# A fused attention and top-2 expert kernel: front reordered, gates and send counts moved into the expert stage, one chain of weight scales, tables read from PSUM

## The reference

```python
xn = _layernorm(x)                      # no scale, no shift, eps 1e-5
# attention, one head, causal, within each batch: q = xn Wq^T + bq, k = xn Wk^T + bk, v = xn Wv^T + bv
# experts:
logits = xn @ Wr + br
probs = softmax(logits)                 # over the 16 experts
topv, topi = top_k(probs, 2)
h = relu(xn @ W1[e] + b1[e])
y = h @ W2[e] + b2[e]
out = x + attention(xn) + sum over the two chosen e of topv * y
```

## Time and profile before

| what | us |
|---|---|
| median of 3 executions | 175.81 |
| lowest, highest | 175.55, 177.71 |
| the profiled execution, its own time | 176.07 |
| its span in the trace | 174.3 |

### The profile page before, as it was taken

The page is one execution under the profiler, slowest core; times in us unless marked ns, Lnnn a source line. Parts: engine busy times, 40 slices in busy tenths (PEclk is TensorE's granted clock), DMA queues, the critical chain, the costliest instruction groups (busy, mean ns, idle before and its releaser), DMA issues.

```text
span 174.3 us, 4762 instructions
## 1 busy us (share of the span) xinstructions
PE 154.9 (89%) x1418; PEld 136.1 (78%) x1418; DVE 113.1 (65%) x447; ACT 114.3 (66%) x337; POOL 99.9 (57%) x149
## 2 busy tenths in 40 slices
PE   5888789998769996989999999999999899987990
PEld 5764444768757855979999999989999799987670
DVE  1589666789997787857988854545453543532772
ACT  3478967897658956119999768786877567464000
POOL 7646888888888886000655565655464645635700
PEclk9999999999999999999999999999999999999999
DMA  5579999610111651154464521001100000003946
GB/s 143 147 262 408 405 406 407 229 46 32 49 47 37 176 139 47 46 127 109 118 151 114 138 78 49 15 9 36 47 32 21 26 30 29 29 34 116 301 140 181
DMA packets 22416, 21.60 MB, mean 124 GB/s; under 512 B 3589, under 2 KB 16211, under 8 KB 22392
## 3 DMA queue, kind: packets, MB, share of 16 engines
q1 hardware_dynamic: 19864, 17.06, 31.1%
q0 software_dynamic: 2528, 4.24, 7.0%
HBM read 14.94 MB, written 7.32 MB: 128 GB/s over the span
## 4 chain that ended last, share of the span: by engine, by line
PE 57%; DVE 19%; issue 8%; DMA 7%; ACT 4%; SPq 1%; POOL 1%; DVEq 0%; POOLq 0%
PE pOO L1201 21%; PE pOO L1093 6%; PE pS L1188 6%; PE pS L1065 6%; PE pS L1190 5%; PE pS L1189 5%; DMA w<-pairs_dram 3%; PE pT L1156 3%; DVE pS L795 3%; DMA pairs_dram<-ybuf,pair 2%; PE pT L1078 2%; DMA xin<-in_L_attn_x 2%; PE pS L986 1%; DVE xin L909 1%; SPq L377 1%
## 5 line engine op out<-in xcount | busy, mean ns | idle before, releaser
L454 POOL DMA_INDIRECT pairs_dram<-ybuf,pair x47 | 46.5, 988 | 50.2 <-DVE ybuf L883 35.9
L580 ACT ACTIVATE xT<-pS,b1t 128x128 f32<-128x128 f32 x188 | 55.1, 406 | 23.1 <-PE pS L1190 22.4
L1201 PE MATMUL pOO<-w,xT 128*128 x376 | 52.0, 282 | 1.0 <-DVE ybuf L883 1.0
L1201 PEld LDWEIGHTS pOO<-w,xT 128*128 128x128 f32 x376 | 45.6, 192 | 1.2 <-issue 1.2
L446 POOL DMA_INDIRECT slots_dram<-rows,slotrow x32 | 31.6, 986 | 9.7 <-POOL tick L448 8.6
L1188 PE MATMUL pS<-xT,w1hi 128*128 128x128 f16 x188 | 33.9, 219 | 1.7 <-DVE xT L876 1.2
L1190 PE MATMUL pS<-xT,w 128*128 128x128 f16 x188 | 33.9, 219 | 0.0
L1189 PE MATMUL pS<-xT,w1hi 128*128 128x128 f16 x188 | 33.9, 219 | 0.0
L875 DVE CAST xT<-pT 128x128 f16<-128x128 f32 x47 | 13.7, 291 | 30.4 <-PE pT L1156 26.8
L1188 PEld LDWEIGHTS pS<-xT,w1hi 128*128 x188 | 21.3, 113 | 3.0 <-DVE xT L876 1.8
L1093 PE MATMUL pOO<-v,probsT 128*128 128x128 f32 x144 | 19.5, 281 | 4.0 <-DVE xin L814 3.6
(11 more groups left out here) (169 smaller groups left out, 230.9 us busy)
## 6 DMA issues: line engine op xcount, KB each, us to landing
w<-in_L_ffn_W SPq DMA_DIRECT2D x8, 1024.0 KB, 8.1
slots<-slots_dram SPq DMA_DIRECT2D x47, 65.0 KB, 1.9
w<-pairs_dram SPq DMA_DIRECT2D x8, 256.0 KB, 4.4
slots_dram<-slots SPq DMA_DIRECT2D x16, 65.0 KB
...
pairs_dram<-ybuf,pair POOLq DMA_INDIRECT x47
slots_dram<-rows,slotrow POOLq DMA_INDIRECT x32
```

The costliest lines, as they stand in the source:

```text
L454: pool.indirect_dma_start(pairs_dram, bass.IndirectOffsetOnAxis(ap=pair[:, j:j + 1], axis=0), ybuf[:, j % NYB, :], None, bounds_check=NT * ...
L580: ins = nc.scalar.activation(hid[:, j % NHB, here], pA(j)[:, here], ACT.Relu, bias=b1t[:, c, j:j + 1])
L1201: ins = pe.matmul(pO[r % 2][:, 0:D], hid[:, r % NHB, c * P:(c + 1) * P], second_weights(r, c), start=(c == 0), stop=(c == NCH - 1))
```

## The change

Front: the normalising of a group is dealt out by tables over ACT, POOL and DVE (group 0: ACT one tile, POOL one, DVE two; group 1: ACT and POOL two each; groups 2 and 3: ACT and DVE two each). On ACT xT_copy(0) moves ahead of std_of(1), qk_copy(1) ahead of xT_copy(1), and qk_copy(3) and v_copy(3) behind the first softmax. On PE project_qk(1) moves ahead of x_transposes(1), project_qk(2) and (3) ahead of x_transposes(2), values(3) behind scores(1), ranks(1), (2), (3) to steps 0, 1 and 5 of the attention, behind attend. On DVE moments(2) moves behind choose(0), inverse_std(2) behind rank(0), logits(3) and rank(1) into the attention. choose(g) loses a conversion and compares the unsigned indices themselves.

Attention: `carry(t)` comes behind `attend(t)`. The weight scales are one chain for 16 experts in step 11 instead of two chains for 8 in steps 7 and 12. hidden_biases and factor_rows are both in step 14; DVE multiplies the biases straight from PSUM (no copy b1raw). Some TENSOR_SCALAR with a scalar from memory become TENSOR_TENSOR with a broadcast. first_rows stands ahead of row_max in step 7.

Experts: the gates leave the attention: DVE subtracts the maxima (`gaps`) in pass 13, ACT takes the exponentials in pass 14, DVE makes the gates in pass 15 and the send counts (`sent_tiles`) in pass 16; ACT's diagonals begin one pass later. LOW_LATE begins with pass 0. SP waits for slotrow_done instead of gates_done, and for sent_done ahead of the counts. lg, oh, at and ex get tiles of their own.

```diff
-    SG = 8
-    WARM_UP = 14
-    ACT_NORMS = 2
+    WARM_UP = 7
+
+    ACT_TILES = [(0,), (0, 1), (0, 1), (0, 1)]
+    POOL_TILES = [(1,), (2, 3), (), ()]
+    DVE_TILES = [(2, 3), (), (2, 3), (2, 3)]
+
+    GATES = 13
+    DIAGS = GATES + 4
 
...
-        SQUARES = {0: (0,), 1: (1,), 2: (2,), 3: (3, 4), 4: (5,), 5: (6, 7), 6: (8, 9), 7: (10, 11), 8: (12,), 9: (13,),
-                   10: (14,), 11: (15,)}
-        HIGH = {8: (0,), 9: (1,), 10: (2,), 12: (3,), 13: (4,)}
-        LOW = {9: (0,), 11: (1,), 13: (2,), 14: (3,)}
+        SQUARES = {0: (0,), 1: (1,), 2: (2,), 3: (3, 4), 4: (5, 6), 5: (7, 8), 6: (9, 10, 11), 7: (12, 13, 14, 15)}
+        HIGH = {12: (0,), 13: (1, 2), 14: (3, 4)}
+        LOW = {13: (0,), 14: (1, 2)}
 
         HIGH_LATE = {j: (j + 5,) for j in range(E - 5)}
-        LOW_LATE = {j: (j + 3,) for j in range(1, E - 3)}
+        LOW_LATE = {j: (j + 3,) for j in range(E - 3)}
 
 
...
-                for t in range(G * g + ACT_NORMS, G * g + G):
+                for t in (G * g + i for i in POOL_TILES[g]):
...
             normalise(0)
+            xT_copy(0)
+            std_of(1)
             act.wait_ge(wT_done, 2)
             nc.scalar.copy(wqkT[:, :, :], pA(2)[:, 0:2 * D].rearrange("p (n d) -> p n d", n=2)).then_inc(wT_copied, 1)
-            std_of(1)
-            xT_copy(0)
             normalise(1)
-            std_of(2)
             v_copy(0)
-            xT_copy(1)
             act.wait_ge(bqk_in, 32)
             qk_copy(0)
+            qk_copy(1)
+            xT_copy(1)
+            std_of(2)
             v_copy(1)
             normalise(2)
-            qk_copy(1)
             xT_copy(2)
             std_of(3)
             qk_copy(2)
             normalise(3)
             v_copy(2)
-            qk_copy(3)
             xT_copy(3)
 
             nc.scalar.activation(loaded[:, :], ident[:, 0:1], ACT.Exp)
-            v_copy(3)
 
             def squares(e):
...
             softmax(0)
+            qk_copy(3)
+            v_copy(3)
+            softmax(1)
             qk_copy(4)
-            softmax(1)
+            probsT_copy(0)
             qk_copy(5)
...
+                if j == GATES + 1:
+                    exponentials()
+                if j == DIAGS:
                     act.wait_ge(gates_done, 1)
-                if E <= j < E + K * NDIAG:
-                    k, t = (j - E) % K, (j - E) // K
+                if DIAGS <= j < DIAGS + K * NDIAG:
+                    k, t = (j - DIAGS) % K, (j - DIAGS) // K
...
-                step(dve.tensor_copy(pickf[:, here, :], pick[:, here, 0:K]))
-                dve.tensor_copy(rows_i[:, here, D + 1], pickf[:, here, 0])
+                dve.tensor_tensor(rows_u[:, here, D + 1], pick[:, here, 0], pick[:, here, 0], ALU.bitwise_or)
                 for k in range(K):
                     ins = dve.tensor_tensor(oh[:, k, here, :], expert_no[:, None, :].broadcast_to([P, G, E]),
-                                            pickf[:, here, k:k + 1].broadcast_to([P, G, E]), ALU.is_equal)
+                                            pick[:, here, k:k + 1].broadcast_to([P, G, E]), ALU.is_equal)
...
             moments(0)
             inverse_std(0)
+            normalise(0)
             moments(1)
             inverse_std(1)
-            moments(2)
             dve.wait_ge(brb_in, 16)
             dve.wait_ge(consts, 1)
             logits(0)
             largest(0)
             choose(0)
-            inverse_std(2)
+            moments(2)
             logits(1)
             rank(0)
+            inverse_std(2)
+            normalise(2)
             moments(3)
             largest(1)
             inverse_std(3)
-            normalise(NG - 1)
+            normalise(3)
             logits(2)
             choose(1)
-            logits(3)
-            rank(1)
 
...
+            def gaps():
+                dve.tensor_tensor(ex[:, :, :], lg[:, :, :], top[:, :, 0:1].broadcast_to([P, NT, E]), ALU.subtract)
+                dve.tensor_tensor(gap[:, :], top[:, :, 1], top[:, :, 0], ALU.subtract).then_inc(gap_done, 1)
...
             row_max(0)
             row_max(1)
+            logits(3)
             largest(2)
             probsT_copy(0)
             row_max(2)
+            choose(2)
             for t in range(NT - 1):
                 if t >= 1:
                     inverse_sum(t - 1)
                     attended(t - 1)
                 probsT_copy(t + 1)
+                if t == 7:
+                    first_rows()
                 if t + 3 < NT:
                     row_max(t + 3)
                 if t == 0:
-                    choose(2)
+                    rank(1)
                 if t == 1:
+                    rank(2)
+                if t == 2:
                     largest(3)
-                if t == 2:
-                    rank(2)
-                if t == 3:
+                if t == 4:
                     choose(3)
-                if t == 4:
+                if t == 5:
                     rank(3)
-                if t == 5:
                     tiles_of_experts()
-                    sent_tiles()
                 if t == 6:
                     experts_of_tiles()
-                    first_rows()
                 if t == 7:
-                    scales(0)
-                if t == 8:
                     rows_of_tiles()
-                if t == 10:
-                    bias_table()
-                    gates()
+                if t == 11:
+                    scales()
                 if t == 12:
-                    scales(1)
-                    dve.wait_ge(scale_done, E // SG)
+                    dve.wait_ge(scale_done, 1)
                     factors()
-                if t == 13:
-                    factor_tables()
                 for e in LOW.get(t, ()):
                     low(e)
+            factor_tables()
             for t in range(NT - LAST, NT):
                 inverse_sum(t)
...
+                if j == GATES:
+                    gaps()
+                if j == GATES + 2:
+                    gates()
+                if j == GATES + 3:
+                    sent_tiles()
...
             values(0)
-            x_transposes(1)
             pe.wait_ge(wT_copied, 2)
             project_qk(0)
-            values(1)
+            project_qk(1)
+            x_transposes(1)
             pe.wait_ge(consts, 1)
             ranks(0)
-            project_qk(1)
+            values(1)
+            project_qk(2)
+            project_qk(3)
             x_transposes(2)
-            project_qk(2)
             values(2)
-            project_qk(3)
             x_transposes(3)
-            values(3)
-            ranks(1)
 
             def tile_rows(bank):
...
                 if t < 2:
-                    project_qk(6 + t)
-                if t == 2:
-                    ranks(2)
-                if t == 4:
+                    ranks(t + 1)
+                if t == 5:
                     ranks(3)
-                if t == 6:
+                if t == 7:
                     pe.wait_ge(total_read, 1)
-                    weight_sums(0, bank)
-                if t == 8:
-                    pe.wait_ge(scale_done, 1)
                     tile_rows(bank)
                 if t == 10:
                     pe.wait_ge(erow_done, 1)
                     pe.wait_ge(onehot_done, 1)
+                    weight_sums(bank)
+                if t == 14:
+                    pe.wait_ge(scale_done, 1)
                     hidden_biases(bank)
-                if t == 12:
-                    pe.wait_ge(b1_read, 1)
-                    weight_sums(1, bank)
-                if t == 13:
-                    pe.wait_ge(scale_done, 2)
                     factor_rows(bank)
...
             scores(0)
             scores(1)
+            values(3)
             project_qk(4)
-            project_qk(5)
             probs_transposes(0)
             scores(2)
+            project_qk(5)
             for t in range(NT - 1):
                 probs_transposes(t + 1)
                 if t + 3 < NT:
                     scores(t + 3)
-                carry(t)
+                if t < 2:
+                    project_qk(6 + t)
                 if t < NT - LAST:
                     attend(t)
+                carry(t)
 
             ids = {}
```

120 lines of the change are left out of this document (51 added, 69 removed).

## The result

Four runs of the changed kernel took 178.7 to 181.27 us, median 181.01; the kernel before, in the same session, 175.55 to 177.71, median 176.25. The ratio is 1.023, with a 95% interval of 1.012 to 1.034. The forecast was 177.6 with a range up to 179.0. The profiled run took 181.27, its span is 179.5.

What follows compares the result with a forecast made beforehand. PE's attention and POOL's strictly serial sends were taken to end together at 74.1, PE bounding the expert stage. Span 174.3 + 0.7 + 1.1 = 176.1, plus 1.77 around it 177.9, less 0.26: 177.6 us; range 175.2 to 179.0.

Steps and rivals of the forecast that it cites:

- Term 1: Front: GpSimd's (POOL's) sends begin 0.35 us later, the first at 16.0, because rank(0) comes later.
- port lock: Front, group 0: DVE's and POOL's normalising instructions exclude each other, up to 0.45 later, 178.05 us in all; chance 0.08.
- Term 2: Attention: ranks(1) comes late on PE, so from group 1 on sends are 1.4 us later, ninth at 30.5, term 1 included.
- ranks in time: Attention: PE or ACT reaches ranks(1) one microsecond sooner; hidden(0) 0.35 earlier than now, 176.6 us in all; chance 0.15.
- a ninth send by 29.5: Group 1's first send: the forecast, which put it at 30.5, called itself wrong if it came by 29.5.
- Term 3: Hand-over to the expert stage: slots land at 75.3, attend(15) loses its 0.59 wait, hidden(0) 0.7 us later than 77.03.
- the attention would end well before the slots: Hand-over: attend(14) done about 73.7, 1.6 us ahead of the slots, so attention edits cost and bring nothing before 75.3.
- Term 4: Expert stage: gates and counts on DVE stall PE 0.6 in pass 18 and 0.5 in 19, 1.1 us; bounds 0 and 1.5.
- neither stalls: Ranks in time and DVE's lateness also absorbed in the expert stage: 175.81 - 0.35 = 175.5 us; chance 0.15.

Runs made afterwards that it cites:

- e13: The changed kernel with SyncE's six send counts asserted in bounds, fourth run, on a fourth chip: 174.38 us, ratio 0.995 to the kernel before.
- e4: The changed kernel with no GpSimd sends in the expert stage; SyncE writes result tiles by plain DMA, scatter by token left out: 192.7 us, ratio 1.101.
- e7: The changed kernel, counts asserted, with GpSimd's memset after each send 176 elements wide instead of 352: 172.37 us, ratio 0.980.
- e12: The changed kernel with SyncE's six send counts asserted in bounds, third run, on a third chip: 173.59 us, ratio 0.989 to the kernel before.
- the controls: Four runs, on four chips, of the changed kernel with SyncE's counts asserted in bounds: 174.62, 175.33, 173.59 and 174.38 us, mean ratio 0.995.
- e9: The kernel before, counts asserted, with only gaps, exponentials, gates and send counts moved to passes 13 to 17 of the expert stage: 175.37 us, ratio 1.004.
- e8: The changed kernel, counts asserted, with gates and send counts spread over passes 15 to 21 and diagonals begun in pass 21: 174.03 us, ratio 0.986.
- e6: The kernel before with its counts asserted and nothing else changed: 175.39 us, ratio 0.9987.
- e1: The changed kernel with SyncE's six send counts asserted in bounds (12 more instructions), first run: 174.62 us, ratio 1.000 to the kernel before.
- e5: The changed kernel with SyncE's six send counts asserted in bounds, second run, on a second chip: 175.33 us, ratio 0.995 to the kernel before.
- e3: The kernel before, counts asserted, with five unread dependent products, some 2.3 us, added on VectorE in pass 15: 175.63 us, ratio 1.001.
- e14: The changed kernel, counts asserted, with six more unread dependent products, 2.7 us, on VectorE behind the gates in pass 15: 179.19 us, ratio 1.026.

## Why the prediction was wrong

**Term 1, first send 0.35 later: right in size, lucky to the tenth.** 16.00, as worked out; in the front also the table load came at 20.9 for 21.1. But one trace could not have shown 0.35: the twelve traces of kernels with the changed front have their first send between 15.52 and 17.88, the four with the old one between 15.46 and 16.06. The medians, 15.95 and 15.62, lie 0.33 apart.

The port lock, which the prediction had as a rival at 0.08, is part of that scatter. VectorE's two normalising instructions and GpSimd's one, first group of the changed kernel, and then the same place in e13 with the two instructions that GpSimd has next:

```profile
5.84 0.66 DVE L622 TENSOR_SCALAR rows<-xin,rstd,nbias 128x128 f32<-128x128 f32 x2
5.91 0.52 POOL L430 TENSOR_SCALAR rows<-xin,rstd,nbias 128x128 f32<-128x128 f32 x1 [0.48 <-DVE nbias L616]
```

```profile
5.76 1.59 DVE L622 TENSOR_SCALAR rows<-xin,rstd,nbias 128x128 f32<-128x128 f32 x2
5.83 0.52 POOL L430 TENSOR_SCALAR rows<-xin,rstd,nbias 128x128 f32<-128x128 f32 x1 [0.40 <-DVE nbias L616]
6.29 0.52 POOL L435 MEMSET b2rows<- 128x512 f32 x1
...
6.75 0.52 POOL L436 MEMSET b1rows<- 128x512 f32 x1
```

Beside a GpSimd that waits, two such instructions on VectorE take 0.60 (at 15.37 in the changed kernel). At 5.84 they take 0.66 and end 0.07 behind GpSimd's; beside a MEMSET (18.62, same trace) they take 0.75 and end 0.08 behind it; in e13 they take 1.59 and end 0.08 behind the second MEMSET. In e4 and e7 it is 1.59 and 1.60 in the same way. So VectorE stood still until GpSimd was done, for 1.0 us in three traces of twelve and for under 0.1 in the other nine. In the three logits(0) comes at 10.09, 10.26 and 11.61, where it is 9.12 to 9.49 in the nine, and the first send at 16.35, 16.53 and 17.88. In e13 the transposes and values(0) on TensorE, begun 0.8 later, also took 1.09 and 2.20 us for 0.67 and 1.25. It is not the only cause of scatter: e12 has 16.43 without it. The rule of the Trainium skill (SBUF — State Buffer, Who interferes with whom), that one of the two blocks for the other's whole instruction, agrees with these rows. The prediction's price for it was 0.45; it left out the two MEMSETs that stand behind GpSimd's tile. What decides between a short and a long block is open.

**Term 2, sends 1.4 later from group 1 on: wrong.** slotrow of group 1 was ready at 28.43 + 0.29 = 28.72, where the sum had 29.55, and the ninth send at 29.53 waited for its tick alone. The step that failed is the addition of rows between softmax(0) and ranks(1), and in it ScalarE's part: softmax(0) began at 22.30 and probsT_copy(0) ended at 25.00, where the sum had 22.5 and 25.9, since each record there begins about 0.1 before the one before it has ended. TensorE's part (2.5 from there to the end of ranks(1)) and VectorE's (1.2) came out as summed. In all it was 0.8 too long, which was most of the 1.05 that the ninth send was to lose by waiting. This was the rival "ranks in time", at 0.15, and the prediction's own sign of being wrong, a ninth send by 29.5, is met but for 0.03. The last send, moreover, did not even keep the 0.35: from the first send to the last it is 51.4, where it was 51.8, in every later trace too (51.4 to 51.5 with the change, 51.7 to 51.9 without it, the kernels with a short tick apart). Most of that is the one long send of the kernel before.

**Term 3, hidden(0) 0.7 later: wrong in sign.** It followed from term 2. With sends in time, the hand-over is what the prediction said of it: the slots bind, with TensorE ready 1.4 before them (1 to 2 was written), and attend(15) loses its wait. hidden(0) came 0.7 earlier in the first pair; the rival had 0.35. Behind the first send it came 1.0 earlier in the first pair and 1.3 to 1.8 in the controls. That the attention would end well before the slots, and that its edits would bring nothing beyond, e9 and e8 show at 2.5 and 3.2 us, and the controls at 0.6 to 1.7.

**Term 4, 1.1 us in the expert stage: wrong in size.** 0.4 in pass 18 for 0.6, and 0.02 in pass 19 for 0.5, and so in every trace with the gates in two blocks (steps of 2.13 or 2.14). The place and the cause were right. hidden(18) would have begun 3.26 behind the CAST of slot 17, as the sum has it; the slot parts it waits for were done at 3.6 for 3.8. In pass 16 they were done at 5.15 for 6.1, with hidden(19) due at 5.4: the counts were costed by their rows in the attention, 1.4, and took 0.84 here, and successive rows overlap by up to 0.1.

Put together with what was measured for each term, the sum is 175.8 - 0.7 + 0.4 = 175.5; the case "neither stalls" had that number, but by luck: it had no stall and 0.35. The controls' mean of 174.5 lies 1 below it, and by their ratio, 0.995, the change makes the kernel 0.5% faster, under what the measurement can tell from nothing on three chips of four.

**What the first session had on top, 6.2 us, no term or rival foresaw**, and it is what carried the time out of the range. The prediction's expert stage takes 1.73 a pass wherever VectorE is in time, that is, it puts the way from the end of a product on TensorE to the ReLU and the CAST at its usual length in every pass. In its place the runs show signals up to 1.9 us late and nine steps of about 2.5. Reading the trace of before more closely would have given a hint: its last passes have the step of 2.44 already, and its ReLU stands 0.90 behind the product.

It belongs to the conditions of that session or to the unasserted counts. For the first: the kernel before had its signals late in the same session, from its first send in the expert stage, and not in e6. And the assertions, which thirteen of the fourteen later kernels have, run at 107.8 to 109.1 in e1 and at 103.2 to 104.5 in e6, while the first late signals on record come at 84.9 in the changed kernel and at 83.9 in the kernel before, when SyncE has done nothing yet that differs between the two forms. So the first lateness is hardly theirs; where the program lies in memory differs too, and no run tests that. The nine steps begin behind that point, and for them the two are not told apart: the changed kernel with unasserted counts was not run again, and of the kernel before, which ran unasserted beside every experiment (174.8 to 176.0 us on five chips), no later trace was kept. Why it hit the changed kernel nine times and the kernel before once is open as well. What the trace shows is that GpSimd's sends mostly stood 1.28 to 1.34 apart in threes in the changed kernel from pass 18 on, and in the kernel before only from pass 40 on, and that signals were held while they did. (In e5 two sends stand 1.29 apart there, with no effect.) That the gates' delay pushed the sends together, and that this with late signals makes the pattern, fits both traces; it was not shown, since no chip since had late signals. Shown is that the delay alone, short (e1, e3) or long (e14), does not do it.
